# Context projections of a decoder layer: the weight cast on ScalarE, memsets of the padding alone, logarithms and scalings between evictions

## The reference

```python
q = (query @ Wq.T + bq) * d ** (-0.5)
k = key_ @ Wk.T + bk
v = value @ Wv.T + bv
scores = jnp.einsum('bhqd,bhkd->bhqk', q, k)
distance_bias = -jnp.log(distances + 1e-09) * jnp.abs(distance_scaling)
scores = scores + distance_bias[:, None, :, :]
attn = jax.nn.softmax(scores, axis=-1)
out = jnp.einsum('bhqk,bhkd->bhqd', attn, v)
```

## Time and profile before

| | us |
|---|---|
| median of 3 runs | 2983.29 |
| lowest, highest | 2980.57, 3001.35 |
| the profiled execution | 3013.61 |
| its span, first to last instruction | 3011.9 |
| the stage within the span | 1970.0 to 2019.5 |

### The profile page before, as it was taken

How to read it: one execution, slowest core, us unless ns; L and a number is a source line. 1 busy time by engine, 2 the same in 40 slices (tenths; PEclk the granted TensorE clock), 3 DMA queues, 4 the chain that set the end, 5 groups by cost and what they waited for, 6 DMA issues and landing times. The chain is left out here.

```text
span 3011.9 us, 43200 instructions
## 1 busy us (share of the span) xinstructions
PE 2729.9 (91%) x14144; PEld 1813.6 (60%) x14145; DVE 2055.6 (68%) x3529; ACT 1413.4 (47%) x2572; POOL 978.0 (32%) x1000
## 2 busy tenths in 40 slices
PE   7989999999999899999998999658998589999995
PEld 6754555555555345555555555446666469788895
DVE  4568878888886588788777887455665457333337
ACT  2215767767677444444444455323444343333335
POOL 4457530000000254334435554451000350343322
PEclk9988999999999899999999999878999789999998
DMA  6999985446350444555555542255664423323425
GB/s 223 316 252 277 246 229 76 67 62 82 54 78 12 98 117 139 155 170 147 148 161 135 144 121 89 99 138 81 110 110 87 133 93 114 135 80 110 170 89 168
DMA packets 246193, 400.03 MB, mean 133 GB/s; under 512 B 37711, under 2 KB 147895, under 8 KB 244727
## 3 DMA queue, kind: packets, MB, share of 16 engines
q1 hardware_dynamic: 177940, 251.20, 31.6%
q10 hardware_dynamic: 49299, 82.70, 13.0%
q0 software_dynamic: 18768, 63.79, 6.8%
HBM read 231.46 MB, written 166.14 MB: 132 GB/s over the span
## 5 line engine op out<-in xcount | busy, mean ns | idle before, releaser
L655 DVE TENSOR_REDUCE an_m<-an_psm 128x1 f32<-128x512 f32 x1024 | 626.2, 682 | 112.1 <-PE an_psm L577 112.1
L639 ACT ACTIVATE an_probs<-an_pst 128x512 f32<-128x512 f32 x1024 | 517.9, 628 | 226.4 <-PE an_pst L605 226.4
L1397 ACT ACTIVATE wj_probs<-wj_pst 128x512 f32<-128x512 f32 x512 | 297.8, 595 | 354.7 <-PE wj_pst L1239 345.5
L1114 POOL TENSOR_TENSOR wj_sums<-wj_sums,wj_probs 128x512 f32<-128x512 f32 x192 | 265.2, 1381 | 321.3 <-ACT wj_probs L1397 318.4
L1428 DVE TENSOR_REDUCE wj_m<-wj_pm 128x1 f32<-128x512 f32 x512 | 324.1, 680 | 17.9 <-PE wj_pm L1214 17.5
L605 PE MATMUL an_pst<-an_qs,an_ks 128*128 128x512 f32 x640 | 264.0, 412 | 10.4 <-ACT an_probs L639 5.7
L577 PE MATMUL an_psm<-an_ks,an_qs 127*128 127x512 f32 x640 | 255.6, 399 | 2.3 <-DVE an_m L655 2.3
L1228 PE MATMUL wj_pacc<-wj_probs,wj_vs 128*64 128x512 f32 x1024 | 250.5, 610 | 2.7 <-ACT wj_probs L1397 2.7
L1239 PE MATMUL wj_pst<-wj_qs,wj_ks 128*128 128x512 f32 x512 | 204.1, 399 | 0.0
L1114 DVE TENSOR_TENSOR wj_sums<-wj_sums,wj_probs 128x512 f32<-128x512 f32 x192 | 180.3, 939 | 20.2 <-ACT wj_probs L1397 20.2
L1154 POOL MEMSET wj_qs<- 64x2048 f32 x2 | 3.5, 1798 | 577.4 <-issue 577.4
(11 more groups left out here) (430 smaller groups left out, 6037.6 us busy)
## 6 DMA issues: line engine op xcount, KB each, us to landing
ew_w<-scr_ws SPq DMA_DIRECT2D x10, 3072.0 KB, 12.1
scr_ws<-wide_pair POOLq DMA_DIRECT2D x27, 1024.0 KB, 5.8
ac_qs<-scr_xq ACTq DMA_DIRECT2D x48, 256.0 KB, 6.1
an_qs<-scr_q SPq DMA_DIRECT2D x40, 256.0 KB, 11.7
an_ks<-scr_k SPq DMA_DIRECT2D x40, 256.0 KB, 13.2
wj_qs<-scr_mq ACTq DMA_DIRECT2D x18, 512.0 KB, 5.2
wj_ks<-scr_mk ACTq DMA_DIRECT2D x18, 512.0 KB, 6.0
scr_xs<-x_acc SPq DMA_DIRECT2D x2, 4128.0 KB, 15.9
```

The source lines that it names most:

```text
L639: act.activation(probs[:, (NSTEP * G + s) % HELD, j], pst[:, (GH * s + j) % RING], ACT.Exp, scale=HD ** -0.5).then_inc(exp_done, 1)
L655: dve.tensor_reduce(m1[:, hq, kh, col:col + 1], psm[:, part % MB], AX.X, ALU.max).then_inc(mx_done, 1)
L1114: eng.tensor_tensor(sums[:, x % CPB, j], earlier, probs[:, s % RING, j], ALU.add).then_inc(sum_done[j], 1)
L1397: act.activation(probs[:, x % RING, j], pst[:, j], ACT.Exp, scale=BHD ** -0.5).then_inc(exp_done, 1)
```

## The change

The cast of the weights moves from VectorE to ScalarE, behind the identity. GpSimd clears only the padding columns of xa, xb and t, in eight memsets; it takes over the clearing of v16 and its ones; distT and distF come behind that, and the memsets of keys go to the end of its list. ScalarE's logarithms stand between the evictions of t, and VectorE's scalings between the evictions of values. The semaphore `zeroed` now counts the eight padding memsets; TensorE waits for four of them ahead of the key units, VectorE for all eight ahead of the casts of t. Two new semaphores, `v_set` and `dist_set`, cover v16 and distT.

```diff
@@ -1632,24 +1632,29 @@
 
         @block.gpsimd
         def _(pool):
-            pool.memset(xa[:].bitcast(F32), 0.0).then_inc(zeroed, 1)
-            pool.memset(xb[:].bitcast(F32), 0.0).then_inc(zeroed, 1)
-            pool.memset(t[:], 0.0).then_inc(zeroed, 1)
-            pool.memset(distT[:], 0.0).then_inc(zeroed, 1)
-            pool.memset(distF[:, :, :, :, E2:].bitcast(F32), 0.0).then_inc(zeroed, 1)
-            pool.wait_ge(zeroed, 5)
+            for kh in range(KH):
+                pool.memset(xa[:, kh, :, E2:].bitcast(F32), 0.0).then_inc(zeroed, 1)
+                pool.memset(xb[:, kh, :, E2:].bitcast(F32), 0.0).then_inc(zeroed, 1)
+            for s in range(len(k_units)):
+                pool.memset(t[:, s, :, E2:], 0.0).then_inc(zeroed, 1)
+            pool.memset(v16[:], 0.0).then_inc(v_set, 1)
+            pool.wait_ge(v_set, 1)
+            pool.memset(v16[0:E2, :, :, HD:HD + 1], 1.0).then_inc(v_set, 1)
+            pool.memset(distT[:], 0.0).then_inc(dist_set, 1)
+            pool.memset(distF[:, :, :, :, E2:].bitcast(F32), 0.0).then_inc(dist_set, 1)
+            for s in range(len(k_units)):
+                pool.wait_ge(a_done, s + 1)
+                pool.tensor_tensor(ab[:, s, 1], t[:, s], ab[:, s, 0], ALU.subtract).then_inc(b_done, 1)
+            for b in range(B):
+
+                pool.wait_ge(scaled, b + 1)
+                pool.tensor_copy(distF[:, b, :, :, 0:E2], dist[:, b].rearrange("p t (e n) -> p t e n", e=2)).then_inc(rounded, 1)
+                pool.wait_ge(rounded, b + 1)
             pool.memset(keys[4 * HD:].bitcast(F32), 0.0).then_inc(keys_set, 1)
             pool.wait_ge(keys_set, 1)
             pool.memset(keys[4 * HD:, :, :, :, 0:E2].bitcast(F32), 1.0).then_inc(keys_set, 1)
             pool.wait_ge(keys_set, 2)
-            for s in range(len(k_units)):
-                pool.wait_ge(a_done, s + 1)
-                pool.tensor_tensor(ab[:, s, 1], t[:, s], ab[:, s, 0], ALU.subtract).then_inc(b_done, 1)
-            for b in range(B):
-
-                pool.wait_ge(scaled, b + 1)
-                pool.tensor_copy(distF[:, b, :, :, 0:E2], dist[:, b].rearrange("p t (e n) -> p t e n", e=2)).then_inc(rounded, 1)
-                pool.wait_ge(rounded, b + 1)
+            pool.wait_ge(dist_set, 2)
 
         @block.tensor
         def _(pe):
@@ -1663,6 +1668,7 @@
                 last.then_inc(px_ready, 1)
             pe.wait_ge(xb_done, len(x_units))
             pe.wait_ge(w_done, 1)
+            pe.wait_ge(zeroed, 2 * KH)
             for n, (j, u) in enumerate(k_units):
                 if n >= 2:
                     pe.wait_ge(t_done, n - 1)
@@ -1687,21 +1693,27 @@
         @block.scalar
         def _(act):
             act.activation(identF[:], ident[:], ACT.Copy).then_inc(ident_done, 1)
-            act.wait_ge(zeroed, 2)
+            act.wait_ge(w_in, 32)
+            act.activation(wa[:], raw[:], ACT.Copy).then_inc(wa_done, 1)
             for n, (kh, u) in enumerate(x_units):
                 act.wait_ge(px_ready, n + 1)
                 act.activation(xa[:, kh, HB * u:HB * u + HB, 0:E2], px[:, n % 2, :, 0:E2], ACT.Copy).then_inc(xa_done, 1)
-            act.wait_ge(s_chain, 1)
-            for b in range(B):
+
+            def logarithm(b):
+
                 act.wait_ge(dist_in[b], 16)
                 act.activation(dist[:, b], dist[:, b], ACT.Ln, bias=tiny[:]).then_inc(ln_done, 1)
+
+            act.wait_ge(s_chain, 1)
             act.wait_ge(small_in, 48)
-            act.wait_ge(zeroed, 3)
             for n, (j, u) in enumerate(k_units):
                 act.wait_ge(k_ready, n + 1)
                 act.activation(t[:, n, :, 0:E2], po[:, n % 2, 0:HB * EP].rearrange("p (e n) -> p e n", n=EP)[:, :, 0:E2],
                                ACT.Identity, bias=kbias[:, j:j + 1]).then_inc(t_done, 1)
-            act.wait_ge(zeroed, 4)
+                if n:
+                    logarithm(n - 1)
+            logarithm(B - 1)
+            act.wait_ge(dist_set, 1)
             for n, (b, e, hq) in enumerate(d_units):
                 if n % 2 == 0:
                     act.wait_ge(pd_ready, n + 1)
@@ -1711,8 +1723,6 @@
         @block.vector
         def _(dve):
             dve.memset(tiny[:], 1e-9).then_inc(s_chain, 1)
-            dve.wait_ge(w_in, 32)
-            dve.tensor_copy(wa[:], raw[:]).then_inc(wa_done, 1)
             dve.wait_ge(wa_done, 1)
             dve.tensor_tensor(wb[:], raw[:], wa[:].bitcast(F32), ALU.subtract).then_inc(w_done, 1)
             for n, (kh, u) in enumerate(x_units):
@@ -1721,28 +1731,26 @@
                 dve.tensor_tensor(xb[:, kh, blocks, 0:E2], px[:, n % 2, :, 0:E2], xa[:, kh, blocks, 0:E2].bitcast(F32), ALU.subtract)\
                     .then_inc(xb_done, 1)
 
-            dve.memset(v16[:], 0.0).then_inc(queries_set, 1)
             dve.memset(queries[4 * HD:].bitcast(F32), 0.0).then_inc(queries_set, 1)
-            dve.wait_ge(queries_set, 2)
-            dve.memset(v16[0:E2, :, :, HD:HD + 1], 1.0).then_inc(ones_set, 1)
             dve.wait_ge(small_in, 48)
             dve.tensor_scalar(negated[:], scaling[:], -1.0, None, ALU.mult).then_inc(s_chain, 1)
             dve.wait_ge(s_chain, 2)
             dve.tensor_tensor(nabs[:], scaling[:], negated[:], ALU.min).then_inc(s_chain, 1)
             dve.wait_ge(s_chain, 3)
-            for b in range(B):
-                dve.wait_ge(ln_done, b + 1)
-                dve.tensor_scalar(dist[:, b], dist[:, b], nabs[:, 0:1], None, ALU.mult).then_inc(scaled, 1)
+            dve.wait_ge(zeroed, 2 * KH + len(k_units))
             for n in range(len(k_units)):
                 dve.wait_ge(t_done, n + 1)
                 dve.tensor_copy(ab[:, n, 0].bitcast(FR), t[:, n]).then_inc(a_done, 1)
-            dve.wait_ge(ones_set, 1)
-            dve.wait_ge(small_in, 48)
-            dve.wait_ge(zeroed, 4)
+            dve.wait_ge(v_set, 2)
             for n in range(NE_):
                 dve.wait_ge(v_ready, n + 1)
                 dve.tensor_tensor(v16[0:E2, n, :, 0:HD], po[0:E2, n % 2, 0:H].rearrange("p (h d) -> p h d", h=NH),
                                   vbias[0:E2].rearrange("p (h d) -> p h d", h=NH), ALU.add).then_inc(v_done, 1)
+                if n % 2:
+                    b = n // 2
+                    dve.wait_ge(ln_done, b + 1)
+                    dve.tensor_scalar(dist[:, b], dist[:, b], nabs[:, 0:1], None, ALU.mult).then_inc(scaled, 1)
+            dve.wait_ge(dist_set, 1)
             for n, (b, e, hq) in enumerate(d_units):
                 if n % 2:
                     dve.wait_ge(pd_ready, n + 1)
```

More of the change, by code:

```diff
@@ L1601, in context_projections @@
         dist_in = [k.sem(f"dist_in{b}") for b in range(B)]
-        names = ("zeroed", "ones_set", "wa_done", "w_done", "s_chain", "ln_done", "scaled", "px_ready", "xa_done",
+        names = ("zeroed", "v_set", "dist_set", "wa_done", "w_done", "s_chain", "ln_done", "scaled", "px_ready", "xa_done",
                  "xb_done", "k_ready", "t_done", "a_done", "b_done", "v_ready", "v_done", "pd_ready", "pd_act", "pd_dve",
                  "stored", "rounded")
-        (zeroed, ones_set, wa_done, w_done, s_chain, ln_done, scaled, px_ready, xa_done, xb_done, k_ready, t_done, a_done,
+        (zeroed, v_set, dist_set, wa_done, w_done, s_chain, ln_done, scaled, px_ready, xa_done, xb_done, k_ready, t_done, a_done,
          b_done, v_ready, v_done, pd_ready, pd_act, pd_dve, stored, rounded) = (k.sem(n) for n in names)
@@ L1652, in _ @@
                 pool.wait_ge(rounded, b + 1)
+            pool.memset(keys[4 * HD:].bitcast(F32), 0.0).then_inc(keys_set, 1)
+            pool.wait_ge(keys_set, 1)
+            pool.memset(keys[4 * HD:, :, :, :, 0:E2].bitcast(F32), 1.0).then_inc(keys_set, 1)
+            pool.wait_ge(keys_set, 2)
+            pool.wait_ge(dist_set, 2)
         @block.tensor
```

## The result

| | us |
|---|---|
| before, median of 20 runs | 2995.23 (2980.57 to 3002.11) |
| after, median of 20 runs | 2986.14 (2967.52 to 2996.65) |
| ratio after to before | 0.9963, 95% interval 0.9947 to 0.9979 |
| the same comparison on another occasion (11 and 22 runs) | 2981.68 to 2998.01, ratio 0.9937, interval 0.9916 to 0.9957 |
| profiled execution of after, its span | 2984.6, 2982.9 |

The change gains 11.1 us by the first ratio (6.3 to 15.9; the medians differ by 9.1), within what I had called no change. The forecast was 11.7 us less, but the time I gave, 2971.6 with a range of 2962 to 2983, is wrong: 2986.1 lies above the range.

The account below looks back on a forecast made before the run. It took the stage (49.5 of 3011.9 us) as bound by waits between engines, chiefly for VectorE's late cast. Its end moves from 2019.1 to 2007.4, 11.7 us less; off the median 2983.3 that gives 2971.6, range 2962 to 2983.

Parts of the forecast that it names:

- I take the same 11.7 off the median: 2971.6: Whole kernel: the stage's 11.7 us gain taken off 2983.3, the median of the three runs shown.
- second base: Whole kernel: profiled execution of 3013.6 us less 11.7 gives 3001.9.
- Beside it GpSimd runs its zeroing back to back: Stage before: VectorE's weight cast lasts 12.64 us beside GpSimd's memsets, ending just after distT's; alone it would take under 1.
- the new critical point: Casts of t on VectorE wait for GpSimd's distT memset until 1984.0; 4 us of the old wait come back.
- From here on scalings and subtractions take turns: After the fourth cast, VectorE's scalings (0.86) each stand behind a GpSimd subtraction or rounding; the last ends at 1995.4.
- plus 0.8 us: Stage end: added to 11.2 us of distance copies, as TensorE's first two pairs may run at the lower clock level.
- the sum of 3.2 us: GpSimd's eight padding memsets replacing the clearing of xa, xb and t: 3.2 us taken, 6.0 as upper bound.
- ports not in the way: Rival 1: scalings on VectorE stand behind nothing; stage ends at 2003.8, 15.3 us less, 2968.0; chance 0.12.
- starvation through GpSimd's chain: Rival 2: fourth cast waits for three subtractions, scalings behind full roundings; 9.4 to 6.5 us less, 2974 to 2977; chance 0.17.
- The third and fourth: Rivals: next stage's loads stay put, no gain, 2983, chance 0.05; next stage's loop at lower clock, 3013 and up, 0.04.
- The rule weighed: Shared ports: forecast's turns let VectorE in between two consecutive GpSimd operations, as the page has it; the memset trace disagrees.

Follow-up runs that it names:

- logs_only: After, with ScalarE's logarithms one eviction of t earlier and nothing else changed; stage 35.1 us.
- woven: As logs_early, with the first four transposed distance units set between the value units on TensorE and VectorE; stage 40.7 us, ratio to before 0.9979.
- cast_only: Before, with only the weight cast moved to ScalarE; stage 42.5 us.
- before_fourth: The kernel before, unedited, profiled a fourth time; stage 42.5 us.
- cast_last: Before, with VectorE's weight cast made to wait for four GpSimd memsets, distT's the last; stage 50.3 us.
- full_sets: After, with xa, xb and t cleared whole in three memsets instead of padding alone; stage 38.0 us.
- dist_late: After, with the memsets of distT and distF moved behind GpSimd's four subtractions; stage 44.2 us.
- logs_early: After, with logarithms one eviction earlier and distT cleared in four memsets, two of them behind the subtractions; stage 39.4 us.

## Why the prediction was right or wrong

**The base: wrong, and with it the time.** "I take the same 11.7 off the median: 2971.6" is the step that failed. The median of three runs, 2983.3, lay 11.9 us under that of twenty, 2995.2; 2995.2 less 11.7 is 2983.5, 2.6 us from the median of after. The prediction had a second base in hand, 3001.9 from the profiled execution; the two lie 30 us apart, and the measured time lies between them. My range had room for the scatter of three runs of after, not for the same scatter in the base. The scatter is outside the stage. Ahead of it lie 1955.9 us in logs_only and 1973.8 in woven, of instructions that no edit touched. The length of `attend_cross` alone went from 324.6 (cast_only) to 344.2 us (before_fourth), and with it TensorE's waits for the row of maxima, cast_only first:

```profile
PE ac_pst L1922 <- DMA ac_qs<-scr_xm: 5.5, 6, 2.3
```

```profile
PE ac_pst L1922 <- DMA ac_qs<-scr_xm: 18.4, 8, 4.4
```

No kernel of mine touched that transfer; 12.9 of the 19.6 us of difference are this row. The rest is TensorE's busy time, 298.1 us at a mean granted clock of 0.96 and 305.0 at 0.94.

**The kernel before: one form taken for the kernel.** "Beside it GpSimd runs its zeroing back to back" is right for the profile I had, and cast_last confirms it at 50.3 us. But it is the rarer form. Against the common one the change gains 7.5 us, not 14.4. With one long form in seven the mean is 8.5 us, inside the first interval (6.3 to 15.9). So the agreement of 11.7 with 11.1 is in part luck: a sum short by 2.7 us for a case that seldom occurs. There was a warning in the rows: in the earlier trace rows the cast waits through memsets issued after it, in the earlier trace rows VectorE gets in between two operations of GpSimd. An outcome that goes both ways in one trace may go both ways in one place.

**The terms against the long form**, in us from the stage's start, forecast and measured in after:

| step | forecast | measured |
|---|---|---|
| wa cast on ScalarE | 1.1 | 1.04 |
| key matmuls start | 5.5 | 5.3 |
| GpSimd's distT memset ends | 14.0 | 13.1 |
| fourth cast of t ends | 16.8 | 16.6 |
| fourth scaling ends | 25.4 | 23.7 |
| last copy of distT ends | 37.4 | 34.8 |

The front of the chain held, and the new critical point was the one named: the casts behind the distT memset. Two terms were mis-sized. "From here on scalings and subtractions take turns" was costed at a whole subtraction in front of each scaling, over 2.1 us a turn; the scalings came 1.6 to 1.8 us apart, each 0.99 to 1.18 us long instead of 0.86, and GpSimd paid with 1.46 to 1.84 us for a subtraction. From the fourth cast to the fourth scaling that is 7.1 us instead of 8.6. The "plus 0.8 us" for the lower clock was not due: the windows of after give a granted clock of 1.00 from the value units on. The pads cost 0.38 us from start to start, and four of t 0.91, so the sum of 3.2 us was 0.8 too high; full_sets shows their worth at 2.9 us.

**The rivals.** The first, ports not in the way, puts the stage at 34.2 us (49.5 less 15.3) and the forecast at 37.8 (49.5 less 11.7). The 35.1 measured lie nearer to the rival, but its reason was wrong: the holds were there. The second, starvation through GpSimd's chain, did not happen in after. A mild form, one subtraction ahead of a cast, is seen in logs_only. The full one is seen in dist_late and logs_early, where memsets stood behind the subtractions, and in the long form of before. The third and fourth fell: the next stage's first matmul came 4.2 us after its start, as before, and its length lies in the scatter of before.

**The rule weighed.** The page "SBUF — State Buffer" of the Trainium skill, section "Who interferes with whom", says that the engine that issues first has the shared ports for its whole instruction, and that the other blocks. With the blocking the runs agree: the cast took 0.69 us alone and 2.28 behind one memset. With the order they do not always agree: in logs_early a scaling issued at 1982.08 let three later memsets pass, and in before the same pair ended either way.

**What stays open.** The second comparison gave 18.9 us, at least 12.9, which the stage's mean gain of 8.5 does not reach. The 8.5 rests on one long form in seven profiles, and none of the 22 executions of before in that comparison was profiled: had all been long, the stage would give 14.4. So a larger share of long forms there is neither shown nor excluded. Outside the stage the ten profiles of before and its three variants have 2955 us on average, the ten of after and its variants 2949, each group scattering by 7 to 9 us; I can't call that a difference. What decides which engine goes next when a memset ends was not found.

## What to carry to other kernels

Before you take a gain off a profile, ask whether the wait in it happens every time: where two engines exclude each other, which goes next may differ from one execution to the next, and a second profile of the same kernel costs little. When VectorE's casts and scalings share a stage with GpSimd, place GpSimd's memsets where VectorE has only subtractions, memsets or reads of PSUM (they kept their 1.22, 3.47 and 0.69 us beside memsets here), and never in a row behind work that VectorE's next scaling is waiting to follow. And put the error of the base, not just that of the gain, into the range of a time.

## What the runs showed that I had not expected

- A VectorE cast or scaling can wait through a row of GpSimd memsets issued after it: 12.64 us for a cast of 0.69 in before, 8.12 us and 5.04 us for a scaling of 0.84 in dist_late and logs_early. Beside the row of subtractions and roundings in after it never waited more than 0.4 us; in logs_only a cast waited some 1.1 us, one subtraction long.
- The same program has two lengths of one stage, 42.4 to 42.8 and 49.5 us, by which engine goes next when GpSimd's first memset ends.
- Cutting a memset in two left no gap for the other engine in logs_early and woven.
- ScalarE clears 128x2048 in 1.89 us with a copy scaled by zero, and beside it a GpSimd memset of that size kept its 1.80 us and a VectorE memset its 3.47.
